# Moving a tile's K/V projection ahead of the first head pair in an attention and FFN kernel

## What is computed

```python
def reference(x, Wq, Wkv, Wproj, w1, b1, w2, b2):        # x: 16 x 2048 x 1024, f32
    x = x + layernorm(attn(layernorm(x), Wq, Wkv, Wproj))
    x = x + layernorm(relu(layernorm(x) @ w1 + b1) @ w2 + b2)   # width 4096
    return x
# attn: 16 query heads, 4 key/value heads, head size 64; q and k divided by their norms
# and rotated (RoPE); softmax(q k^T / 8) over the last 512 positions, causal; times v; @ Wproj.T
```

## Time and profile before

| | us |
|---|---|
| median of 2 runs | 4560.22 (4544.31 and 4576.13) |
| the profiled execution | 4543.13 |
| span of its slowest core (core 2) | 4541.6 |
| spans of the eight cores | 4536.4 to 4541.6 |
| PE busy | 2574.5 (57%) |
| DVE busy | 1748.0 (38%) |
| ACT busy | 1259.7 (28%) |

### The profile page before, as it was taken

How to read it: one execution, slowest core, us unless ns; L and a number is a source line. 1 busy time by engine, 2 the same in 40 slices (tenths; PEclk the granted TensorE clock), 3 DMA queues, 4 the chain that set the end, 5 groups by cost and what they waited for, 6 DMA issues and landing times.

```text
span 4541.6 us, 50176 instructions; the slowest of 8 cores (4536.4 to 4541.6 us)
## 1 busy us (share of the span) xinstructions
PE 2574.5 (57%) x15614; PEld 1261.1 (28%) x15808; DVE 1748.0 (38%) x4530; ACT 1259.7 (28%) x4001; POOL 9.4 (0%) x21
## 2 busy tenths in 40 slices
PE   2444545545554545545545537676667666676676
PEld 1222333333332223323323322222222222222222
DVE  2343343343344433333433423333333333333333
ACT  1344444444443444444444430000000000000000
POOL 0000000000000000000000000000000000000000
PEclk7666666666666666666666658888888888888888
DMA  7000000000000000000000130000000000000000
GB/s 136 19 10 19 10 10 17 12 10 16 13 10 19 10 19 10 10 19 10 10 19 10 29 74 10 19 19 19 19 19 19 19 19 19 19 19 19 19 19 19
DMA packets 20723, 93.12 MB, mean 21 GB/s; under 512 B 2336, under 2 KB 2352, under 8 KB 19056
## 3 DMA queue, kind: packets, MB, share of 16 engines
q1 hardware_dynamic: 18432, 67.12, 4.3%
q0 software_dynamic: 2032, 22.79, 3.0%
HBM read 78.89 MB, written 33.55 MB: 25 GB/s over the span
## 4 chain that ended last, share of the span: by engine, by line
PE 41%; DVE 24%; issue 14%; ACT 8%; DVEq 6%; DMA 4%; ACTq 2%; SPq 0%; POOL 0%; POOLq 0%
PE psO L714 6%; DVE sb_aT L573 6%; PE ptr L682 5%; DVEq L797 5%; PE psX L714 5%; DVE sb_hT L686 5%; PE pjq L365 4%; PE psAV L591 3%; PE pjq L634 3%; PE ptr L563 3%; DMA sb_xt<-x 3%; PE psE L696 3%; DVE sb_st L253 3%; ACT sb_junk L515 2%; PE ptr L276 2%
## 5 line engine op out<-in xcount | busy, mean ns | idle before, releaser
L563 PE MATMUL ptr<-sb_ident,sb_E 128*128 128x128 bf16 x2240 | 289.5, 278 | 722.4 <-DVE sb_aT L573 719.8
L686 DVE TENSOR_SCALAR sb_hT<-ptr,sb_b1f 128x128 bf16<-128x128 bf16 x1024 | 290.5, 284 | 521.9 <-PE ptr L682 521.1
L682 PE MATMUL ptr<-sb_ident,sb_hT 128*128 128x128 bf16 x1024 | 232.2, 227 | 418.4 <-DVE sb_hT L686 248.5
L276 PE MATMUL ptr<-sb_ident,sb_ln 128*128 128x128 bf16 x512 | 64.8, 307 | 638.1 <-DVE sb_ln L270 593.5
L563 PEld LDWEIGHTS ptr<-sb_ident,sb_E 128*128 128x128 bf16 x2240 | 177.9, 120 | 814.9 <-issue 806.3
L591 PE MATMUL psAV<-sb_aT,sb_VR 128*64 128x128 bf16 x2240 | 320.4, 298 | 88.9 <-DVE sb_aT L573 88.8
L573 DVE COPY sb_aT<-ptr 128x640 bf16<-128x640 bf16 (+4 forms) x720 | 263.3, 366 | 237.8 <-PE ptr L563 213.1
L682 PEld LDWEIGHTS ptr<-sb_ident,sb_hT 128*128 128x128 bf16 x1024 | 100.9, 99 | 752.7 <-issue 752.7
L262 ACT ACTIVATE sb_st<-sb_st,sb_epsc 128x1 f32<-128x1 f32 x128 | 37.7, 295 | 906.9 <-DVE sb_st L258 906.9
L696 PE MATMUL pjq<-sb_warena,sb_lt 128*128 128x512 bf16 x993 | 286.8, 392 | 1.9 <-DVE sb_lt L282 1.3
L714 PE MATMUL psO<-sb_warena,sb_hT 128*128 128x512 bf16 x993 | 275.7, 442 | 3.6 <-issue 2.6
(11 more groups left out here) (124 smaller groups left out, 4378.0 us busy)
## 6 DMA issues: line engine op xcount, KB each, us to landing
sb_xt<-x SPq DMA_DIRECT2D x32, 512.0 KB, 4.1
sb_warena<-w POOLq DMA_DIRECT2D x8, 2048.0 KB, 47.6
x1s<-sb_x1t SPq DMA_DIRECT2D x32, 512.0 KB, 2.9
sb_x1t<-x1s SPq DMA_DIRECT2D x32, 512.0 KB, 4.1
y<-sb_xt SPq DMA_DIRECT2D x32, 512.0 KB, 2.8
sb_warena<-wq POOLq DMA_DIRECT2D x1, 2048.0 KB, 26.7
sb_warena<-wp POOLq DMA_DIRECT2D x1, 2048.0 KB, 38.6
sb_warena<-wkv POOLq DMA_DIRECT2D x1, 1024.0 KB, 15.5
```

What stands on the lines that cost most here:

```text
L276: E("pe", lambda e, c=c: e.transpose(ptr[:, c * 128:(c + 1) * 128], src_ap_fn(c), ident[:]), reads=(src_tag, "ident"), writes=("ptr",))
L563: E("pe", lambda e, eb=eb, jj=jj, slot=slot: e.transpose(ptr[:, slot * 128:(slot + 1) * 128], eb[:, jj * 128:(jj + 1) * 128], ident[:]), r ...
L682: E("pe", lambda e, m=m, slot=slot: e.transpose(ptr[:, slot * 128:(slot + 1) * 128], hTb[:, m * 128:(m + 1) * 128], ident[:]), reads=(f"{h ...
L686: E("dve", lambda e, m=m, slot=slot: e.tensor_scalar(hTb[:, m * 128:(m + 1) * 128], ptr[:, slot * 128:(slot + 1) * 128], b1f[:, m:m + 1], ...
```

## The change

The dictionary `sched` says ahead of which pair a piece is emitted. Piece 0, `kv_mms`, moves from pair 1 to pair 0. In the list it now stands behind the layer norm and the transposes of the next tile and ahead of the current tile's first scores. All else stays.

```diff
-            sched = {1: [0], 2: [1], 3: [3], 4: [4], 5: [5], 6: [2]} if INTERLEAVE else {}
+            sched = {0: [0], 2: [1], 3: [3], 4: [4], 5: [5], 6: [2]} if INTERLEAVE else {}
```

## The result

| | before | after |
|---|---|---|
| median, us | 4544.7 (10 runs) | 4721.2 (11 runs) |
| lowest, us | 4543.3 | 4713.6 |
| ratio | | 1.0371 (95% interval 1.0348 to 1.0395) |

The account below looks back on a forecast made before the run. Waits along a PE, DVE and ACT chain set the time, no engine being full. 23 x 5.02 = 115 plus 34 gave 149 us on 4543.1, 4692; 6 us for the median made 4698, range 4655 to 4742.

Parts of the forecast that it names:

- Step 1: K/V block in an attention tile: starts no earlier, 2.2 us after the transposes in both kernels, since it needs lt.
- step 2: K/V block ahead of pair 0's scores: lasts 3.50 us, so those scores start 4.76 us late.
- Step 3: Hole left ahead of pair 1: gives nothing back in 23 steady tiles, pair 1 4.77 us late.
- Step 4: Pair 1's scores fall to the low clock: 0.25 us more, so a steady tile loses 5.02 us.
- Rival A: Clock rises inside the K/V block, making it 2.71 us: 3.5 us lost a tile, 4650 us; chance 0.08.
- Step 5: Eight short tiles (0 to 3 old key tiles): 3.1, 4.0, 4.8 and 5.0 us late, 34 us in all.
- Step 6: Later parts of a tile, with the query blocks: taken as nothing, 1.2 us a tile either way kept for the range.
- rival B: Query blocks and projection on the low clock oftener: 1.2 us more in 31 tiles, 37 us, 4735; chance 0.07.
- within 2%: Whole time not told apart from no change: rest of A, D and most of C, chance put at 0.07.

Follow-up runs that it names:

- the run without the wait: Changed kernel, with the moved K/V matmuls reading the other, long-ready lt buffer (the current tile's), so they don't wait for the copies; median 4665.9 us of two runs.
- the run with half the block: Against the kernel before: four of the eight K/V matmuls ahead of pair 0's scores, four ahead of pair 1's; 4642.2 us, ratio 1.0205.
- the changed kernel with one square: Changed kernel plus one unused 1.1 us square of x on ACT per tile, ahead of the next tile's layer norm statistics; 4716.6 us.
- the one with only pair 0 moved ahead: Against the kernel before: pair 0's scores ahead of the next tile's layer norm and transposes, K/V block still ahead of pair 1; 4538.6 us, ratio 0.9968.
- three squares: Kernel before plus three unused squares of x on ACT per tile, ahead of the next tile's layer norm statistics; 4637.9 us, ratio 1.0204.
- block behind pair 1: Against the kernel before: K/V block moved behind pair 1's scores, layer norm and transposes left in place; 4631.0 us, ratio 1.0167.
- five squares: Kernel before plus five unused squares of x on ACT per tile, ahead of the next tile's layer norm statistics; 4734.8 us, ratio 1.0409.
- The kernel with one square: Kernel before plus one unused square of x on ACT per tile, ahead of the next tile's layer norm statistics; 4583.2 us, ratio 1.0084.
- The faster kernel: Against the kernel before: pair 0's scores ahead of the next tile's layer norm and transposes, K/V block behind pair 1's scores; 4413.5 us, ratio 0.971.

## Why the prediction was right, and where it was short

- Step 1 (the block starts no earlier) and step 2 (3.50 us) were right: the block starts at +2.21 and takes 3.50. The two parts are shown apart by the run without the wait (1.35 of the 4.76 us is the wait) and the run with half the block.
- Step 3 (the hole gives nothing back) was right. The delay was 4.77 us at pair 0's first exp (+6.63 against +1.86), and leaving the block out of the kernel before gains nothing.
- Step 4 (0.25 us for the low clock) was right: the wait is 0.49 us in the tile shown, and pair 0 to pair 1 takes 5.52 us on average and took 5.27. The granted clock was 1.00 under pair 1's scores before, and is 0.50 from pair 1 to pair 2 now. The rule of the Trainium skill ("TensorE: Matmul & The Clock Gate", section "HAM oscillation — how this bites in real kernels") that gaps send the array back to the slow clock agrees with this only in the outcome: the clock was already at 0.50 in the block ahead of PE's gap of 3.47 us, so here the gap did not lower it.
- Rival A (the clock rises in the block) held in 2 of the 21 tiles averaged here, where pair 0's scores came at +5.3 to +5.4 and the tile was some 89.4 us long. In the others they came at +5.71, as with a block at the low clock from end to end. Keeping block and scores together did not as a rule bring the full clock.
- Step 5 (short tiles, 34 us) was right: pair 1's first exp came 2.9, 3.4 to 3.7, 4.6 to 4.8 and 4.8 to 4.9 us later, for 3.1, 4.0, 4.8 and 5.0; 32 us in all.
- Step 6 (later parts of the tile) is the term that was mis-sized. It was put at nothing, and up to 1.2 us a tile were kept for the range (rival B). The two query stretches cost 1.1 us more per steady tile on average, 1.7 in the tile shown. 23 tiles of it are 25 us, and the sum lacked 171 - 149 = 22 us. So what came is the forecast with nearly all of rival B, and the total, 4721, lies between the two. That the 4698 is only 23 us short is in part luck: it holds 6 us for the median before, which stood 17 us above the profiled execution with two runs. Over ten runs that median is 4544.7, 1.6 us above it. Without the 6 us the forecast is 4692, 29 us short. Some 5 of these are the difference between the medians (176.5) and core 5's traces (171); the cores differ by more than that, and no run looks at it.
- That the sign of step 6 could not be told from the trace of before was fair, as the runs show: the same order with one more microsecond has the short query stretches again. What could have been seen there is that they were mostly short already: of 21 steady tiles 18 took 9.0 to 9.4 us from pair 2 to 3, one 9.9 and two 10.4. That pointed to a cost above nothing. But it is not shown that the kernel before was at its best: from pair 3 to 4 it mostly took 8.9 to 9.0 us, and the changed kernel with one square took 7.4 there in 5 of its 21 tiles.
- The chances have a slip in their sum: the forecast, B and half of A are 0.79 + 0.07 + 0.04 = 0.90, not 0.92, which leaves 0.09 and not 0.07 for "within 2%".

What stays open: what fixes where in a tile the clock rises. The runs show that added work moves the query blocks on and off the full clock, that it isn't the block's old place that matters, and that length alone doesn't settle it. No run changed the clock by itself, so that the low clock causes these 1.1 us is read from the stretches (the same work on ACT and DVE, a lower clock, a longer time) and not shown by an experiment. What is shown is that they come and go with added work in either order.

## What to carry to other kernels

What matters is ahead of which instruction of a queue a block stands, and not only whether its engine has room: ask what the engine behind it will be doing meanwhile. Work for a later tile belongs behind the scores that feed ACT, and best just behind, so that ACT's own work covers it; work that needs nothing from a load belongs ahead of what waits for that load. A price that goes with the clock (here some 1.1 us a tile) should be taken as a cost, not as nothing, if most tiles of the kernel before already show the short time.

## What the runs showed of the hardware

In many of these kernels the tile lengths gathered. On the slowest core the median steady tile is 85.4 us in the kernel before and in the one with only pair 0 moved ahead; 88.7 to 88.8 in four others (three squares, half the block, no wait, block behind pair 1); and 92.0 to 92.2 in three (the changed kernel, the same with a square, five squares), though what was added to them differs by a microsecond and more within each of the last two groups. It is no rule without exceptions. The kernel without the block has 85.8 with several tiles of 87.4 to 88.0. The kernel with one square has 87.8 on its slowest core, of tiles of some 86 and some 88 us, and 85.8 to 86.3 on the others. The faster kernel's tiles range from 78.4 to 82.5 us. Why the lengths gather is not settled by these runs.

A microsecond of ACT work was nearly free in the changed kernel (4717 against 4721) and cost slightly more than itself in the kernel before (39 us for 34). So a comparison of two orders that differ by a microsecond a tile can come out either way; the stretch that pays is seen only if its granted clock is read beside its length.
